# Where GpSimd stops between its first gathers, and who makes one quad's inner pairs, in a recommendation tower on one core

## What is computed

```python
e = jnp.stack([tbl_0[ids[:, 0]], ..., tbl_15[ids[:, 15]]], axis=1)      # x: 2048 x 16 x 256
for i in range(3):
    z = einsum('bfe,bge->bfge', x, xk)          # all 256 pairs of fields
    z = relu(einsum('bcl,oc->bol', z, Ws[i]) + bs[i][None, :, None])
    z = sum(z, axis=-1)                         # 16 numbers a sample
    xk = broadcast_to(z[:, :, None], x.shape)
h = concatenate([z of the 3 layers, dense_ctx], axis=1)                 # 64 numbers
h = max(h @ W_top1 + b_top1, 0); h = max(h @ W_top2 + b_top2, 0); y = h @ W_top3
```

## Time and profile before

| | before |
|---|---|
| median of 3 runs | 588.89 us (588.57 to 591.03) |
| profiled execution, its own time | 585.98 us |
| its span | 583.9 us |
| VectorE (DVE) busy | 551.2 us, 94% |
| ScalarE (ACT) busy | 484.3 us, 83% |
| TensorE (PE) busy | 481.0 us, 82% |
| GpSimd (POOL) busy | 472.2 us, 81% |
| mean granted clock of TensorE | 0.956 |

### The profile page before, as it was taken

The page is one execution under the profiler, slowest core; times in us unless marked ns, Lnnn a source line. Parts: engine busy times, 40 slices in busy tenths (PEclk is TensorE's granted clock), DMA queues, the critical chain, the costliest instruction groups (busy, mean ns, idle before and its releaser), DMA issues.

```text
span 583.9 us, 10751 instructions
## 1 busy us (share of the span) xinstructions
PE 481.0 (82%) x4014; PEld 195.5 (33%) x4014; DVE 551.2 (94%) x326; ACT 484.3 (83%) x1427; POOL 472.2 (81%) x354
## 2 busy tenths in 40 slices
PE   6559778786878788898889789788979888798988
PEld 6214223232323333243332324233333323233344
DVE  1698999999999999999999999999999999899995
ACT  1143678999898999989898998989999998989776
POOL 6676888878888888888888888888888888886911
PEclk9589997899999999899999979999999989889999
DMA  3352221212222222222212212212222222120000
GB/s 97 92 151 66 74 64 45 73 56 59 70 66 57 59 73 63 57 64 72 56 55 73 65 55 64 74 54 56 73 65 56 63 73 58 58 68 1 2 1 0
DMA packets 14332, 35.41 MB, mean 61 GB/s; under 512 B 5493, under 2 KB 5879, under 8 KB 14266
## 3 DMA queue, kind: packets, MB, share of 16 engines
q0 software_dynamic: 12288, 33.57, 20.1%
q1 hardware_dynamic: 1994, 1.17, 0.8%
HBM read 34.71 MB, written 0.01 MB: 59 GB/s over the span
## 4 chain that ended last, share of the span: by engine, by line
DVE 46%; PE 20%; ACT 19%; issue 12%; another core or an unknown queue 2%; DMA 1%; POOL 1%; ACTq 0%; DVEq 0%
DVE prod L409 36%; PE z_ps L801 11%; ACT outer L610 10%; DVE outer L457 7%; PE t_ps L764 3%; ACT sq L555 2%; ACT relu L566 2%; ACT outer L600 2%; ACT xt L547 2%; PE zs_ps L816 1%; DVE intra L422 1%; PE turn_ps L834 1%; PE turn_ps L865 1%; PE turn_ps L873 1%
## 5 line engine op out<-in xcount | busy, mean ns | idle before, releaser
L409 DVE TENSOR_TENSOR prod<-t_ps,xt 128x2048 f32<-128x2048 f32 x190 | 420.6, 2282 | 10.8 <-remote 6.6
L323 POOL DMA_INDIRECT x_rows<-in_tbl,ids_sb x256 | 248.0, 969 | 76.4 <-issue 67.6
L610 ACT ACTIVATE outer<-outer,bias_sb 128x256 f32<-128x256 f32 x487 | 241.7, 515 | 6.8 <-DVE outer L457 4.5
L801 PE MATMUL z_ps<-prod,w_sb 128*32 128x512 f32 x1520 | 189.1, 612 | 37.5 <-DVE prod L409 30.6
L337 POOL TENSOR_TENSOR intra<-xt 128x1024 f32<-128x1024 f32 (+4 forms) x90 | 210.0, 2352 | 9.7 <-ACT xt L547 4.8
L457 DVE TENSOR_TENSOR outer<-y_ps,z_all 128x1536 f32<-128x1536 f32 (+2 forms) x66 | 110.5, 1717 | 4.2 <-ACT outer L600 3.4
L547 ACT ACTIVATE xt<-t_ps 128x512 f32<-128x512 f32 x128 | 74.8, 599 | 45.1 <-remote 24.2
L610 ACT ACTIVATION_READ_ACCUMULATOR outer<-outer,bias_sb 128x1 f32 x487 | 100.9, 207 | 0.0
L764 PE MATMUL t_ps<-ident,x_rows 128*128 128x128 f32 x512 | 82.1, 291 | 16.9 <-DMA x_rows<-in_tbl,ids_sb 5.5
L801 PEld LDWEIGHTS z_ps<-prod,w_sb 128*32 128x32 f32 x1520 | 46.4, 111 | 125.4 <-issue 95.6
L764 PEld LDWEIGHTS t_ps<-ident,x_rows 128*128 128x128 f32 x512 | 57.0, 145 | 78.5 <-issue 59.8
(11 more groups left out here) (61 smaller groups left out, 203.9 us busy)
## 6 DMA issues: line engine op xcount, KB each, us to landing
x_rows<-in_tbl,ids_sb POOLq DMA_INDIRECT x256
w_sb<-in_w SPq DMA_DIRECT2D x1, 512.0 KB
feat<-in_dense SPq DMA_DIRECT2D x1, 128.0 KB
w_sb<-in_w SPq DMA_DIRECT2D x1, 128.0 KB
ids_sb<-in_ids SPq DMA_DIRECT2D x1, 120.0 KB
ident<-in_identity SPq DMA_DIRECT2D x1, 64.0 KB, 2.1
w_sb<-in_w0t SPq DMA_DIRECT2D x1, 64.0 KB
sel_sb<-in_sel SPq DMA_DIRECT2D x1, 48.0 KB
```

The source lines that it names most:

```text
L323: pool.indirect_dma_start(out=x_rows[:, par, f, :], out_offset=None, in_=tables[f], in_offset=bass.IndirectOffsetOnAxis(ap=ids_sb[:, NF * ...
L409: dve.tensor_tensor(prod[:, m % PROD_RING, half, :].rearrange("p (f g s) -> p f g s", f=QF, g=QF), t_ps[:, tbank(b, q, half), :, :].unsque ...
L610: act.activation(outer[:, o // OP, o % OP, :], outer[:, o // OP, o % OP, :], ACT.Relu, bias=bias12_sb[:, layer - 1, o:o + 1], accum_out=z_ ...
L801: mm = pe.matmul(z_ps[j * GR:(j + 1) * GR, m % 2, 0:n], w0_sb[:, half, slot, :], src[:, half, j * n:(j + 1) * n], start=(slot == 0 and hal ...
```

## The change

GpSimd's list for the first two batches is rewritten; from batch 2 on the loop is as it was.

- The stops. Before, GpSimd waits behind 12 gathers (for batch 0's tile (1,1)), 16 (tile (2,1)), 20 (tile (3,0)), 24 (tile (3,1)), 28 (contraction of u2) and 32 (batch 1's tile (0,1)). Now it waits behind 8 gathers (batch 0's tile (1,1)), 12 (tile (2,1)), 20 (contraction of u2) and 24 (batch 1's tile (1,1)).
- Batch 0's third quad. Its inner pairs, which VectorE made behind u2, are made by GpSimd behind the 16th gather (`inner_pairs_filled`), with a semaphore of their own, `intra_filled`. TensorE waits for it before batch 0's i1, ScalarE before it overwrites `xt` in batch 2.
- Batch 1's fourth quad and the first two quads of batch 2 are now gathered between batch 1's inner pairs, and the first quad of batch 3 behind them.

```diff
+POOL_FIRST = 2
...
+            def inner_pairs_filled(q):
+
+                pool.wait_ge(copied, tile(0, q, 1) + 1)
+                x = xt[:, 0, :, q * QF:(q + 1) * QF, :].rearrange("p h i s -> p h (i s)")
+                at = 0
+                for d in (1, 2, 3):
+                    n = (QF - d) * P
+                    pool.tensor_tensor(intra[:, q // 2, :, q % 2, at:at + n], x[:, :, 0:n], x[:, :, d * P:d * P + n],
+                                       ALU.mult).then_inc(intra_filled, 1)
+                    at += n
...
             pool.wait_ge(ids_first, 16)
             gather(0, 0, 2 * QF)
+            pool.wait_ge(transposed, tile(0, 1, 1) + 1)
             gather(0, 2 * QF, 3 * QF)
-            pool.wait_ge(transposed, tile(0, 1, 1) + 1)
+            pool.wait_ge(transposed, tile(0, 2, 1) + 1)
             gather(0, 3 * QF, NF)
-            pool.wait_ge(transposed, tile(0, 2, 1) + 1)
+            inner_pairs_filled(POOL_FIRST)
             pool.wait_ge(ids_loaded, 16)
             gather(1, 0, QF)
-            pool.wait_ge(transposed, tile(0, 3, 0) + 1)
+            pool.wait_ge(contracted, part(0, "u2") + 1)
             gather(1, QF, 2 * QF)
-            pool.wait_ge(transposed, tile(0, 3, 1) + 1)
+            pool.wait_ge(transposed, tile(1, 1, 1) + 1)
             gather(1, 2 * QF, 3 * QF)
-            pool.wait_ge(contracted, part(0, "u2") + 1)
+            inner_pairs(1, 0, (1,))
             gather(1, 3 * QF, NF)
-            pool.wait_ge(transposed, tile(1, 0, 1) + 1)
-            gather(2, 0, QF)
-            for b in range(1, NB):
+            inner_pairs(1, 0, (2, 3))
+            gather(2, 0, 2 * QF)
+            inner_pairs(1, 1, (1,))
+            gather(2, 2 * QF, 3 * QF)
+            inner_pairs(1, 1, (2, 3))
+            gather(2, 3 * QF, NF)
+            gather(3, 0, QF)
+            for b in range(2, NB):
                 inner_pairs(b, 0, (1,))
...
                 multiply(b, 2)
-                if b == 0:
-                    inner_pairs_first(2)
                 outer_pieces(b - 1, 1)
...
                     if b == 2:
-                        act.wait_ge(intra_first, 3 * NQ)
+                        act.wait_ge(intra_first, 3 * (NQ - 1))
+                        act.wait_ge(intra_filled, 3)
...
                     if b == 0:
-                        pe.wait_ge(intra_first, 3 * 2 * (pair + 1))
+                        pe.wait_ge(intra_first, 3 * (pair + 2))
+                        if pair == POOL_FIRST // 2:
+                            pe.wait_ge(intra_filled, 3)
```

More of the change, by code:

```diff
@@ L124, in build @@
         intra_first = sem("intra_first")
+        intra_filled = sem("intra_filled")
         intra_done = sem("intra_done")
```

## The result

| | before | after |
|---|---|---|
| median | 588.89 us (588.57 to 592.84, 7 runs) | **594.86 us** (593.01 to 595.57, 7 runs) |
| ratio to before | | **1.0096**, 95% interval 1.0075 to 1.0116 |
| profiled execution, span | 585.98, 583.9 us | 594.85, 593.1 us |
| granted clock of TensorE | 0.956 | 0.945 |

What follows compares the result with a forecast made beforehand. VectorE (94% busy) bounds the kernel, with GpSimd nearly full and living on its lead. A GpSimd lag of 8.7 us costs 4.3 to 7.4, middle 6.0: 588.89 + 6.0 = 594.9 us; range 590.2 to 599.5.

Steps and rivals of the forecast that it cites:

- The start: Batches 0 and 1: first product at 16.3 instead of 19.88, batch 1's first at about 54.2, only 0.4 us gained.
- The 3.5 us said to be lost at the start: Batch 0's outer product starts at 71.3 instead of 67.83, as batch 1's fourth quad comes later.
- the 9.7 and the 11.9 of the prediction: TensorE, from square to batch 1's second quad's tiles: 11.9 us before, 9.7 with the square at full clock.
- The upper end of 54.4: Batch 1's second quad transposed by 54.4, not 52.5, if idle TensorE is held at half clock; adds 1.9 us.
- GpSimd's lag: From batch 1's inner pairs on, GpSimd is 1.0 + 10.0 - 2.3 = 8.7 us late, eight gathers being added work.
- L: Theory that GpSimd's lag behind VectorE decides; for 7.1 us of lag alone it expected 3.5 to 6.5 us slower.
- in every batch: Sign: from about batch 5 on, VectorE waits for ScalarE's slices in every batch, some 0.5 us each.
- The chain behind the inner pairs: Batch 12's inner pairs to VectorE's outer product: 9.6 us, 0.7 to spare, or 8.4; product up to 7.4 us late.
- (a): Late first signal has another cause: first product stays at 19.9, 597.7 us; chance 0.20, shared with both delays.
- (b): TensorE reaches batch 1's second quad near 49, lag about 5, loss 1 to 2.9, near 591 us; chance 0.15.
- (c): Batch 1's first product 5.4 us sooner and GpSimd's lag under 1.3 us: 583.5 us; chance 0.07.

Runs made afterwards that it cites:

- second pair of profiles: Kernels before and after, both unchanged, run and profiled again: medians 589.78 and 594.48 us, after's ratio to before 1.0090.
- e6: Kernel before, with GpSimd making batch 2's first product three times (7.1 us of lag, no gather moved): 593.58 us, ratio 1.0078.
- e2: Kernel before's start up to the 24th gather, then only the stop for batch 1's tile (1,1) and the moved gathers: 583.98 us, ratio 1.0164.
- e11: Kernel before, with gather bursts of 5, 5, 4, 2, the two behind each batch's last inner pairs: 586.11 us, ratio 0.9976.
- e10: Kernel after, three of four gathers from batch 2 on replaced by GpSimd products writing zeros, on a chip with late signals: 585.79 us, ratio 0.9935.
- e1: Kernel after's start, with the eight moved gathers put back ahead of batch 1's first inner pairs as before: 581.57 us, ratio 1.0134.
- e4: Kernel after, three of four gathers from batch 2 on replaced by GpSimd products writing zeros, on the chip without late signals: 583.99 us, ratio 1.0171.

## Why the prediction was right, and where it was not

The time, 594.9 against 594.86, is closer than its reasoning, and that is luck. The sum was made on the profiled execution and gave 592.0; the profile after took 594.85, a loss of 8.9 us between the two profiles and not 6.0. It fits because the execution profiled before lay 2.9 us under its median, and the one after lay on it. In the second pair of profiles (589.78 and 594.36) the loss is 4.6.

**The start: right.** First product 16.01 (predicted 16.3), second unit 25.01 after a wait of 2.65 (25.7, 3.2), GpSimd's three products 3.73 us (3.9), second quad of batch 1 transposed by 51.92 (52.5), batch 1's first product 53.61 (54.2), batch 1's fourth quad 66.69 (66.3), outer product 70.11 (71.3). Two things in the next frame were not priced: the wait of 1.96 us for batch 1's third quad, whose gathers now begin only at 52.19, and the 3.82 us, instead of 1.89, of VectorE's inner pairs at 86.64. The 3.5 us said to be lost at the start were 2.3 at the outer product and 4.2 by batch 2. Of the clock, the square's contraction took 2.95 us, where the earlier trace rows had 3.64 at a granted clock of 0.50. The mean of its stretch is 0.63:

```profile
41.50:44.50 3.00, 2.98 (x17) 0.61 (x18) 3.00 (x3) 0.52 (x1) 2.39 (x3) 0.63 0.40 105
```

That is no third level: the mean granted clock was 0.89 in the first us, from 41.50 on, and 0.50 in each of the two us behind it. So TensorE did fall to the lower level (1.2 GHz), after it had idled for 2.21 us before 40.72, but it started the square at the upper one. The stretch from the square to the second quad's tiles took 10.4 us, between the 9.7 and the 11.9 of the prediction. The fall to the lower level agrees with the Trainium skill (TensorE: Matmul & The Clock Gate, What's actually happening), by which an idle TensorE is held at half its clock. The upper end of 54.4, which was taken to follow from that rule, did not come.

**GpSimd's lag: right.** First inner pairs at 58.12 (57.7) with 28 gathers ahead, batch 2's at 99.13 (99) without a wait, batch 12's last end at 466.87 (466.5). e6 shows that a lag alone costs what L says, e2 that the moved gathers cost 10.3 us on the chip where the start was not in need of help. The sign "in every batch" was not met: VectorE waits for the slices in 7 places from batch 2 on, and elsewhere for tiles.

**The chain behind the inner pairs: the step that failed.** "By the chain as it was (9.6 us and 0.7 to spare)", or 8.4 where it shortens, the slices had to follow the inner pairs of batch 12. They followed by 12.65 us, and the outer product started at 479.56, 10.9 us behind the 468.69 of before, not 4.3 to 7.4. The step took for granted that all other inputs of the chain are ready when the inner pairs come late. They were not: TensorE started i1 3.13 us behind them (0.63 before), after ScalarE had waited 2.17 us for the sum that was seen 1.6 us late. Then i1's own signal was held for 1.34 us (0.05 before), until 1.1 us after the burst of gathers right behind the inner pairs. From there to the slices it took 6.7 us instead of 8.0. Together that is the 2.4 us by which 12.65 exceeds the 10.2 of before. That bursts are what holds the signals is shown for i1's own by e11, where a burst of two does not hold it, and for nearly all of them by e10. How many of TensorE's 3.1 us come from held signals was not measured by itself; in e2, where none is held, TensorE follows by 0.05 us in most batches from 4 on. It was in the trace of before, whose batches 6 to 10 have the same 12.6 to 13.1 us; I had looked at batches 0 and 12 only, at the start and where the chain was 10.2.

**The rivals.** (a) *The stop cures nothing* is false on the chip of the forecast, as the 16.01 shows, and true on the chip of e1 to e4. There the Trainium skill (SBUF — State Buffer, Who interferes with whom), by which a DMA never contends with a compute engine, agrees with the runs: no signal is late. Its rule is on the ports of SBUF, and of signals it says nothing. On the other chips, some 40% of the signals near a gather are, and there the measurement stands against what the prediction drew from that rule. (b) *The lag is small* fell with 58.12. (c) *Faster* needed the lag under 1.3 us; it was 9.1 at batch 12.

## What to carry to other kernels

An engine that is almost full lives on its lead. Work that is moved behind its first product is paid for in the last batch, however idle the start looked, and a stop that saves 3.9 us at the first product can be worth 1.0 at the second batch and less than nothing at the end. Before handing products from GpSimd to VectorE, or moving them, look at which of the other's products they will run beside. Price a stretch of waits from the batch where it is steady as well as from the first and the last. What lies right behind a signal's producer, here a burst of DMA issues on another engine, can be part of the signal's delay, so try a short burst where a signal starts the critical chain, and measure it: here the signal came on time, but the bursts that grew elsewhere held others, and the gain of 1.1 us stayed within the noise.

## What the runs showed of the hardware

- In all runs but e1 to e4 about 100 to 125 of TensorE's signals (7 in e10) arrive over 0.3 us late, all of matmuls that end while GpSimd issues a gather or less than 1.8 us after it. In the kernel after, 44 of 104 arrive within the burst and 56 of them 0.8 to 1.35 us after its last gather. On the chip of e1 to e4 no signal is late. The kernel before takes 573.68 us on that one and 587.2 to 589.1 on the others; without three of four gathers the two kinds of chip are 1.8 us apart. That the late signals make this difference fits e4 and e10 but was not shown.
- What holds a signal (the data transfers, GpSimd's descriptor work or something else) was not separated; e10 took both away together.
- The same three products of VectorE, reading `xt` and writing `intra`, took 1.88 to 1.95 us in 55 cases and 2.1 to 4.6 in the 13 in which a product of GpSimd ran beside them.
